# Another order of maxima, tile work and transposes in an attention kernel, and separate places for one feed-forward block

## The reference

```python
x = x + L0_attn(layernorm(x))   # 8 heads of 64, keys and values from one latent of rank 64:
                                # kv = x @ Wkv_down.T; k = kv @ Wk_up.T; v = kv @ Wv_up.T
                                # softmax(q k^T / 8) v, then @ Wo.T
x = x + L0_ffn(layernorm(x))    # silu(x w1) * (x w2), gelu(h1), gelu(h2), w3; ternary weights, 1024 wide, with scales
x = x + L1_attn(layernorm(x))   # 16 heads of 16, rotary positions, softmax(q k^T / 4) v, then @ wo.T
x = x + L1_ffn(layernorm(x))    # silu(x wg) * (x wu), then wd; int8-valued weights / 127, 768 wide
```

## Time and profile before

| | us |
|---|---|
| median of 3 runs (lowest, highest) | 2413.9 (2413.8, 2413.95) |
| the profiled execution, own time | 2416.73 |
| its span | 2415.0 |
| PE busy in the span | 2335.1 |
| DVE, ACT, POOL busy | 1512.1, 1344.8, 1045.6 |
| granted TensorE clock, mean | 0.992 |

### The profile page before, as it was taken

The page is one execution under the profiler, slowest core; times in us unless marked ns, Lnnn a source line. Parts: engine busy times, 40 slices in busy tenths (PEclk is TensorE's granted clock), DMA queues, the critical chain, the costliest instruction groups (busy, mean ns, idle before and its releaser), DMA issues. The chain is left out here.

```text
span 2415.0 us, 39030 instructions
## 1 busy us (share of the span) xinstructions
PE 2335.1 (97%) x15265; PEld 1450.2 (60%) x15265; DVE 1512.1 (63%) x1934; ACT 1344.8 (56%) x1787; POOL 1045.6 (43%) x674
## 2 busy tenths in 40 slices
PE   6989999999999999999999999999999999999899
PEld 4545555555555788888888887444444444443588
DVE  6877777787784224312322223779989889998364
ACT  3555555554444444444444443478778778778643
POOL 1656776766677346556556556030000000000354
PEclk8999999999999999999999999999999999999999
DMA  1221321321212445555555556434333323332132
GB/s 45 77 69 54 97 77 57 97 68 56 66 49 69 148 166 181 176 193 183 175 192 186 175 195 190 122 89 85 85 76 74 91 70 72 92 84 47 60 119 82
DMA packets 156836, 259.04 MB, mean 107 GB/s; under 512 B 37004, under 2 KB 97292, under 8 KB 156300
## 3 DMA queue, kind: packets, MB, share of 16 engines
q1 hardware_dynamic: 156652, 256.53, 35.6%
HBM read 206.52 MB, written 60.68 MB: 111 GB/s over the span
## 5 line engine op out<-in xcount | busy, mean ns | idle before, releaser
L1839 DVE TENSOR_REDUCE m_mraw<-m_R 128x2 f32<-128x1024 f32 x512 | 622.7, 1221 | 71.7 <-PE m_R L129 60.6
L1690 ACT ACTIVATE m_P<-m_R 128x1024 f32<-128x1024 f32 x512 | 523.6, 1025 | 152.1 <-PE m_R L129 151.9
L584 ACT ACTIVATE a_P<-a_S 128x1024 f32<-128x1024 f32 x256 | 248.7, 1023 | 215.2 <-PE a_S L129 214.2
L129 PE MATMUL m_O<-m_P,m_V 128*17 128x256 f32 x4096 | 330.7, 395 | 4.4 <-ACT m_P L1690 2.5
L882 POOL TENSOR_TENSOR a_accp<-a_accp,a_P 128x1024 f32<-128x1024 f32 x96 | 251.6, 2621 | 15.2 <-ACT a_P L584 6.0
L1944 POOL TENSOR_TENSOR m_act0l<-m_xf,m_act0h 128x512 fp32r<-128x512 f32 x128 | 164.8, 1290 | 212.3 <-ACT m_xf L1752 112.9
L129 PE MATMUL a_O<-a_P,a_V 128*64 128x512 f32 x1024 | 247.7, 605 | 4.4 <-ACT a_ON L592 4.4
L129 PE MATMUL m_R<-m_act0h,wt 128*128 128x512 f32 x640 | 251.4, 393 | 0.2 <-DMA wt<-wcopy 0.2
L129 PE MATMUL m_R<-m_act0l,wt 128*128 128x512 f32 x640 | 250.4, 391 | 0.0
L715 DVE TENSOR_REDUCE a_mraw<-a_X 128x2 f32<-128x1024 f32 x164 | 199.8, 1218 | 78.6 <-PE a_X L129 78.6
L129 PE MATMUL m_R<-m_Q,m_K 64*128 64x512 f32 x800 | 200.6, 498 | 2.5 <-DVE m_mraw L1839 2.2
(11 more groups left out here) (246 smaller groups left out, 4232.7 us busy)
## 6 DMA issues: line engine op xcount, KB each, us to landing
wt<-wcopy SPq DMA_DIRECT2D x176, 512.0 KB, 3.4
m_K<-bounce_k SPq DMA_DIRECT2D x96, 128.0 KB, 5.4
m_ln_x<-x SPq DMA_DIRECT2D x23, 512.0 KB, 4.2
a_tile<-in_L_ffn_tiles SPq DMA_DIRECT2D x22, 512.0 KB, 4.5
wcopy<-in_L_ffn_tiles SPq DMA_DIRECT2D x22, 512.0 KB, 5.2
x<-xres SPq DMA_DIRECT2D x78, 128.0 KB, 3.1
m_Q<-bounce_q SPq DMA_DIRECT2D x150, 64.0 KB, 2.2
xres<-x SPq DMA_DIRECT2D x64, 128.0 KB, 2.7
```

The source lines that it names most:

```text
L129: return pe.eng.matmul(out, lhsT, rhs, start=start, stop=stop, skip_group_check=True)
L584: act.eng.activation(P[n % NP][:, :, :], psS[n % 2][:, :, :], ACT.Exp, scale=SCALE).then_inc(s_exp)
L1690: act.eng.activation(P[h % 4][:, :, :], pair(key)[:, :, :], ACT.Exp, scale=SCALE).then_inc(R.free(key))
L1839: dve.eng.tensor_reduce(mraw[u % 2][:, at, :], pair(key)[:, :, :], AX.X, ALU.max).then_inc(R.free(key))
```

## The change

1. Prologue: of the first norm's eight tiles ACT scales four, ahead of the weight copies, and DVE the other four, ahead of its low parts; PE's first transpose waits for all eight.
2. Eight maxima (those of unit 0) stand before the first turn, not twelve. The four that are missing then are caught up in turns 0 to 3, with three each, the middle one between the scores of the turn's two steps (`taken_in`). The row of unit 1 is asked for in turn 3 instead of turn 2. `EARLY`, the reductions that must have left the banks of `a_S` before the first scores, goes from 8 to 5.
3. In every turn DVE takes the second maximum and the residual before the tile's operation.
4. PE weighs the first step of the turn before ahead of the transposes, the second behind them.
5. ACT copies `a_O` of the previous unit before it rounds a tile.
6. Last feed-forward, block 1: its normed input goes to two parts of `KT[0]` (`m_K`), its norm to half steps LAST - 8 and LAST - 5, its transposes to step 4 of block 0 instead of step 6. ACT and DVE wait, for writing there, for the last scores that read `KT[0]`.

```diff
         self.x = p.sb("ln_x", [128, n, D])
+        self.other_parts = {}
         self.hi, self.lo = parts or [p.sb(f"ln_{x}", [128, 2, n * 128], F32R) for x in ("hi", "lo")]
...
         self.minus_half = p.sb("ln_minus_half", [128, self.n])
+    def parts(self, i):
+        return self.other_parts.get(i, (self.hi, self.lo))
...
         act.wait_ge(*ring.filled(key))
-        act.eng.activation(self.hi[:, f, 512 * half:512 * half + 512], banks[ring.slot(key)][:, :], ACT.Copy).then_inc(self.s_hi)
+        act.eng.activation(self.parts(i)[0][:, f, 512 * half:512 * half + 512], banks[ring.slot(key)][:, :], ACT.Copy).then_inc(self.s_hi)
...
         banks, ring = self.home(i)
-        dve.eng.tensor_tensor(self.lo[:, f, cols], banks[ring.slot(key)][:, :], f32(self.hi[:, f, cols]),
+        hi, lo = self.parts(i)
+        dve.eng.tensor_tensor(lo[:, f, cols], banks[ring.slot(key)][:, :], f32(hi[:, f, cols]),
                               ALU.subtract).then_inc(ring.free(key))
...
     TAIL = [(B - 1, t) for t in range(NT // 2, NT)]
-    EARLY = 8
+    EARLY = 5
     LOWS0, LOWS, LOW_FIRST = 22, 27, 3
...
     def rows_at(u, j):
-        return u + 1 if j == 2 and u + 1 < NU else None
+        return u + 1 if j == (2 if u else 3) and u + 1 < NU else None
...
+    def taken_in(m):
+        first, behind = [min(STEPS, NT + 3 * i, 2 * (i + AHEAD)) for i in (m, m + 1)]
+        return list(range(first, behind))
     def x_order():
...
         out += [("q", u) for u in range(2)] + [("values", 0)]
-        for n in range(2 * AHEAD):
-            out += [("max", n)] if early_banks(n) is None else []
-            out += [("rows", 0)] if n == NT - 1 else []
+        out += [("max", n) for n in range(NT) if early_banks(n) is None] + [("rows", 0)]
         pending = None
         for m, (u, j) in enumerate(turns()):
-            n = 2 * (m + AHEAD)
-            out += [("max", n), ("max", n + 1)] if n < STEPS else []
+            out += [("max", n) for n in taken_in(m)]
             out += [("out", *pending)] if pending else []
...
-        return n % 3 - 1 if n < 2 * AHEAD and n % 3 else None
+        return n % 3 - 1 if n < NT and n % 3 else None
...
             act.eng.activation(wkd[0][:, :, :], raw_d, ACT.Copy).then_inc(s_whi)
+            norm.scale_act(act, 0, 0, 4)
             act.wait_ge(s_prod, 1)
...
                     act.eng.activation(to, psS[i][:, k, 0:256].rearrange("p (g n) -> p g n", g=NG), ACT.Copy).then_inc(s_whi)
-            norm.scale_act(act, 0, 0, NT)
             for i in range(4):
...
                     norm.scale_act(act, norm_at(u, j)[0], 4 * half, 4 * half + 4)
+                if j == 0 and u:
+                    keep_out(u - 1)
                 if tile_at(u, j) and tile_at(u, j)[1] == "round":
                     tile_high(tile_at(u, j)[0])
-                if j == 0 and u:
-                    keep_out(u - 1)
             keep_out(NU - 1)
...
                 norm_step(0, i)
+            norm.scale(dve, 0, 4, NT)
             dve.wait_ge(s_whi, 1)
...
-            for n in range(2 * AHEAD):
+            for n in range(NT):
                 reduce(n)
...
             for m, (u, j) in enumerate(turns()):
-                ahead = 2 * (m + AHEAD)
-                if ahead < STEPS:
-                    reduce(ahead)
+                for n in taken_in(m)[:-1]:
+                    reduce(n)
                 if m:
...
                         add(n)
+                for n in taken_in(m)[-1:]:
+                    reduce(n)
+                if pending:
+                    residual(*pending)
                 if tile_at(u, j):
                     tile_low(*tile_at(u, j))
-                if ahead < STEPS:
-                    reduce(ahead + 1)
-                if pending:
-                    residual(*pending)
                 pending = out_at(u, j)
...
             pe.wait_ge(s_ident, 16)
+            pe.wait_ge(norm.s_scaled, NT)
             for i in range(4):
...
             values(0)
-            for n in range(2 * AHEAD):
+            for n in range(NT):
                 maxima(n)
-                if n == NT - 1:
-                    max_rows(0)
+            max_rows(0)
             pe.wait_ge(s_fill, 7)
...
             for m, (u, j) in enumerate(turns()):
-                ahead = 2 * (m + AHEAD)
-                if ahead < STEPS:
-                    maxima(ahead)
+                for n in taken_in(m)[:1]:
+                    maxima(n)
                 scores(2 * m)
+                for n in taken_in(m)[1:-1]:
+                    maxima(n)
                 scores(2 * m + 1)
-                if ahead < STEPS:
-                    maxima(ahead + 1)
+                for n in taken_in(m)[-1:]:
+                    maxima(n)
                 if pending:
...
                     max_rows(rows_at(u, j))
+                if m:
+                    weigh(2 * m - 2)
                 if turn_at(u, j):
...
                 if m:
-                    for n in (2 * m - 2, 2 * m - 1):
-                        weigh(n)
+                    weigh(2 * m - 1)
                 if way_at(u, j) is not None:
...
     C_PIECES = [START + i for i in (15, 16, 18, 19, 20, 21)]
+    D_SECOND = (LAST - 8, LAST - 5)
     D_LOAD, D_PIECES, D_TURN = LAST - 90, [LAST - 70 + 3 * i for i in range(6)], (LAST - 24, LAST - 20)
...
         k, s = last_at(H) or (NB, 0)
-        return k + 1 if k + 1 < NB and s == LT else None
+        return k + 1 if k + 1 < NB and s == (LT if k else LT - 2) else None
...
         k, s = last_at(H) or (NB, 0)
-        if s in (0, 2) and k + 1 < NB:
+        if s in (0, 2) and 0 < k < NB - 1:
             return norm_of["d", k + 1], int(s == 2)
+        if H in D_SECOND:
+            return norm_of["d", 1], D_SECOND.index(H)
         return None
...
         KT = [p.sb(f"K{i}", [128, 2, T], F32R) for i in range(2)]
+        norm.other_parts = {norm_of["d", 1]: [KT[0][:, :, 512 * i:512 * i + 512] for i in range(2)]}
         QT = [p.sb(f"Q{i}", [128, 2, 512], F32R) for i in range(3)]
...
                 eng.wait_ge(*X.filled(("values", k, 3)))
+            elif i == norm_of["d", 1]:
+                eng.wait_ge(*R.filled(("scores", 16 * (NU - 2) - 1)))
             else:
...
                     for j, w in enumerate(last_gate_weights(m, which)):
-                        for part, x in enumerate((norm.hi, norm.lo)):
+                        for part, x in enumerate(norm.parts(norm_of["d", k])):
                             terms = (w, x[:, j, :]) if exact else (f32(w), f32(x[:, j, :]))
...
                     ins.then_inc(Dr.full(key))
```

## The result

Medians of 13 runs each: 2426.78 us after (2420.47 to 2435.51) against 2414.39 before (2413.25 to 2420.24), ratio 1.0048, interval [1.0038, 1.0057]. The forecast was 2400 with 0.91 on faster; the kernel became 12.4 us slower, outside the range.

The account below looks back on a forecast made before the run. PE was taken as the bound, busy 97% (2335.1 of 2415.0 us), so mainly its waits could go: -3.5 (prologue) + 3.1 (first turns) - 9.7 (steady turns) - 3.8 (last feed-forward) = -13.9 us, giving 2400 us, range 2390 to 2410.

Parts of the forecast that it names:

- (p): Prologue: scaling split between ACT and DVE ends the last low part earlier; -3.5 us, bounds -2.5 and -4.0.
- (f): First turns: scores start 3.4 us earlier, but bank waits and a later row cost more; +3.1 us, bounds +1 and +6.
- (a): Steady turns: copying the weighted sum ahead of the tile's rounding shortens three PE waits by 0.95 each; -2.8 us.
- (b): Steady turns: transposes between the weighting's halves lose their waits, at +0.25 in each of 7 turns for banks; -2.5 us.
- (c): Steady turns: tile operation last on DVE removes a third of 15 us of bank waits; -4.4 us.
- (l): Last feed-forward: block 1's earlier norm and transposes remove PE's wait of 3.74 us; -3.8 us, bounds -3.0 and -4.0.
- sign of failure: Steady turns: the forecast is wrong if turns with a tile operation get longer from 180 us on.
- Rival 4: Tile operation, now last, holds up the next turn's first reduction and second maxima wait, in half the turns; 2428 us; 5%.
- Rival 1: Steady turns: DVE sets the pace with tile operations, the maxima's waits only move, steady part -3; 2406.7 us; 27%.
- Rival 2: First turns: PE stays at 1.2 GHz until turn 4, +10 us on the forecast; 2410 us; 7%.
- Rival 3: Steady turns: tile operation meets no POOL addition, bank waits nearly all go (15 instead of 4.4); 2390 us; 9%.

Follow-up runs that it names:

- one-input kernel: The full change, but DVE's two-input tile subtraction replaced by a one-input reduction of the same size; 2397.61 us, ratio 0.9922 to the kernel before.
- quiet turn: The full change with LOW_FIRST 5 for 3, so every tile step comes two turns later; 2403.01 us, ratio 0.9942 to the kernel before.

## Why the prediction was wrong, step by step

| step | forecast | in the trace of after | alone on the chip |
|---|---|---|---|
| prologue (p) | -3.5 | -2.7 (34.65 for 37.38) | -5.0 |
| first turns (f) | +3.1 | +3.8 | +3.1, no change not excluded |
| copy first (a) | -2.8 | waits 4.4 to 2.0 | +1.0, no change not excluded |
| weighting split (b) | -2.5 | transposes' waits 4.4 to 0.2, latents' 1.1 to 5.3 | +3.0, no change not excluded |
| tile last (c) | -4.4 | third turns +29.4 | +8.7; +14.7 beside the others |
| last feed-forward (l) | -3.8 | -5.5 | -4.4 |

**The step that failed is (c)**, forecast at -4.4 us and measured at +8.7 alone and +14.7 beside the others, by its sentence that the operation's "new place meets another POOL instruction as often as not". How often the two meet did not change at all: in before 19 of the 22 subtractions were stretched, in after 19. What counts is how much of POOL's instruction is left when DVE starts. Over five traces (before, after, the change without (c), (c) alone, (p) and (l)) 96 of the 110 float tiles' subtractions start while POOL's instruction is on record as running. In 89 of them 0.1 us or more of it is left, and there the duration is, to 0.01 us, that rest plus 1.08 us. Of the seven with less left, six take 1.21 to 1.23, and one, at 285.97 of after, waits for POOL's next addition, which starts 0.01 us behind it, and takes 3.47. In before the stretched ones take 1.93 us in the mean (a rest of 0.85), in after 2.70 (a rest of 1.62). And this could be read ahead, in the trace of before, DVE and POOL in the turn that was compared above:

```profile
302.65 2.38 POOL L879 TENSOR_TENSOR a_accp<-a_P 128x1024 f32<-128x1024 f32 x1
302.83 0.17 DVE L728 TENSOR_REDUCE a_mneg<-a_mraw 128x8 fp32r<-128x16 f32 x1
302.93 0.75 DVE L179 BATCH_NORM_STATS2 a_ln_stat<-a_ln_x 128x6 f32<-128x256 f32 x2
```

The new place is right behind the negated maxima, at 302.93, and 0.28 us ahead of it POOL starts an addition of 2.38: 302.65 + 2.38 - 302.93 + 1.08 = 3.18 us, where in its old place it took 1.60 (from 299.95). The forecast took the stretching as a tax with even odds, where it is a wait for one given instruction with a given start. Its own sign of failure came true: the turns with a tile operation got longer, most of them from 180 us on.

**Rival 4 had the place and the sign** (the operation, last, holds up the next turn's first reduction and the second maximum waits for it), with 5%. Its counter-argument, "these turns show hardly any wait, so DVE has slack", was the second error: the slack was 1.9 us of scores against a subtraction of 1.2; it does not hold against one of 2.8 to 3.3 plus 0.75 to 1.0 us of the norm's statistics. Its time of 2428 is near the 2426.8 measured, in part by luck: it took 0.9 us in half of the 54 turns, where the loss is 29.4 in third turns alone, more than half of it in five of them, and 9.7 come back in others. (Its 2449 for all turns leaves out the 4.4 of (c) that its 2428 has.) That the harm is not the order by itself, as rival 4 had it, is shown by the one-input kernel (2397.6) and by the quiet turn (2403.0). Whether the order by itself gains the 4.4 of the forecast in the old turn stays open, since one input was not run with the old order; what is shown is that it gains together with the quiet turn (2407.0 against 2417.5) and that it is worth 39 us there.

**Rival 1** (the waits only move, 27%) had 11 us of bank waits left between 570 and 718; they fell to 5.5, and the loss was elsewhere. **Rival 2** put the clock in the first turns; there it was 1.00 from 41 us on, but in the change without (c) and in the one-input kernel, with the same instructions and nearly the same waits in these turns, it fell to 1.2 GHz for 3.4 us at 48.5 and 47.8, and turn 4 came 1.6 and 1.2 us later than in after. So that part of rival 2 could happen and is not priced in the forecast. In after the clock fell instead in four later third turns and at the latent of unit 14, each time behind a single wait of 1.8 to 2.3 us, as the windows above show for one of them; three more waits of 1.7 to 1.9 us had no fall behind them. This is a part of the loss beyond the waits: the low stretches after 60 and before 760 us sum to 20.5 us of 1.2 GHz in after and none in before, about 10 us of full-speed work. The one-input kernel has 3.4 us of it there. **Rival 3** (the operation meets no addition, 2390) did not happen in the change, where 19 of 22 meet one, but it is what the one-input kernel and the quiet turn brought about, at 2397.6 and 2403.0.

**(b)** had the price (the banks) in the wrong place: 0.25 in each of seven turns, where the latent's matmuls just behind take it at once, 1.83, 1.78 and 1.74 us in units 6, 14 and 22:

```profile
186.03 0.50 PE L129 MATMUL a_X<-a_ln_hi,a_wkd 128*128 128x512 f32 x1 [1.83 <-DVE a_mraw L723]
```

**(a)** had its own waits right, but not its price: it put the later rounding under ACT's waits for scores, and missed that DVE's subtraction waits for that rounding. **(p)**, **(f)** and **(l)** were right in mechanism and near in size: the first scores came 37.78 - 34.65 = 3.1 us behind the negated maxima (2.9 forecast), and PE waited 0.39 to 0.48 twice in turns 2 and 3 (0.65 forecast, or 0.70 by its own numbers, 1.95 - 1.25). The waits of 1.35 in turn 1 and 0.99 at turn 4 were not forecast.

The three wrong terms together: (a) + (b) + (c) were to give -9.7 and gave, by the runs with single parts, about +12.7. All six single parts add up to +6.4, against +12.4 for the change: the other 6 us are (c) beside the rest, 14.7 instead of 8.7.

**The Trainium skill**, in "SBUF — State Buffer", section "SBUF: two separate sides", states the rule: VectorE, with two inputs in SBUF, and GpSimd, with an instruction that reads SBUF, contend for a shared port pair, and it is "an exclusive lock, not a bandwidth split"; whoever starts first has it for the whole instruction. The trace agrees in both directions: 3.33 us for a subtraction that starts 0.13 behind an addition of 2.38, and 5.63 for two additions of 2.38 behind it; and a reduction with one input takes 1.21 beside the same POOL addition. It does not fit the recorded starts everywhere: at 87.53 of after POOL's addition has started 0.36 us ahead of a two-input addition of DVE, and yet DVE's takes 1.21 and POOL's 3.82. Read with the earlier trace rows, it would have made (c) a question of start times instead of odds.

## What to carry to other kernels

When an operation with two SBUF inputs is moved on DVE, look up in the timeline which GpSimd instruction is running at its new start and how much of that is left; here the new duration was that rest plus 1.08 us, against 1.21 alone. The time it costs does not show where it is spent but one bank round later, so compare turns one by one, by their place in the unit, before looking at sums of waits. And a reordering that loses may only stand in the wrong turn: shifting the whole step by two turns changed one number and 24 us. The two have to be tried together: with the old order the same shift cost 29 us.
